# A graph network kernel: the halves of an edge chunk are taken from the two halves of the edge list, each stream of writes waits only for its own, and 23 chunks instead of 30 stand beside the sort

## The reference, cut to what matters

```python
def _L0_gnn_ref(h, row, col, Wq, bq, ...):          # row = src, col = dst
    q = (h @ Wq + bq) * scaling; k = h @ Wk + bk; v = h @ Wv + bv   # 8 heads of 32
    s = einsum('ehd,ehd->eh', q[row], k[col])
    p = exp(s - segment_max(s, row)[row])
    attn = p / segment_sum(p, row)[row]
    return segment_sum(attn[:, :, None] * v[col], row).reshape(n, 256) @ Wo + bo

def _L1_gnn_ref(vertex_features, edge_features, edge_index, W1, ...):
    aggr = segment_sum(edge_features, edge_index[1], num_segments=6250)   # by dst
    h = relu(concatenate([vertex_features, aggr], -1) @ W1 + b1)
    h = relu(h @ W2 + b2)
    return h @ W3 + b3

x = x + _L0_gnn_ref(relu(layernorm(x)), src, dst, ...)
x = x + _L1_gnn_ref(relu(layernorm(x)), edge_attr_256, stack([src, dst]), ...)
```

## Time and profile before

| | |
|---|---|
| median of 3 runs | 1761.8 us (1758.71 to 1763.22) |
| the profiled execution's own time | 1765.26 us |
| its span in the profile | 1763.4 us |
| busy share of the span | PE 82%, DVE 79%, POOL 54%, ACT 44% |
| granted TensorE clock, mean | 0.915 |
| moved by DMA | 431.44 MB, mean 245 GB/s |

### The profile page before, as it was taken

How to read it: one execution, slowest core, us unless ns; L and a number is a source line. 1 busy time by engine, 2 the same in 40 slices (tenths; PEclk the granted TensorE clock), 3 DMA queues, 4 the chain that set the end, 5 groups by cost and what they waited for, 6 DMA issues and landing times.

```text
span 1763.4 us, 26250 instructions
## 1 busy us (share of the span) xinstructions
PE 1450.6 (82%) x7084; PEld 893.7 (51%) x7084; DVE 1394.7 (79%) x2414; ACT 774.4 (44%) x2475; POOL 958.9 (54%) x1021
## 2 busy tenths in 40 slices
PE   4998989965788888877888787876799987778998
PEld 4544444433455555544555455544566655545555
DVE  9998777756777877777878677867898998987785
ACT  5844444445456455545555455520122211115553
POOL 7044444366667666666666566665777777740000
PEclk9999999968989889898989888888999998889999
DMA  9634666688879888889889788876899977763552
GB/s 226 108 117 160 209 210 212 208 281 306 304 262 315 287 291 309 302 297 308 296 274 314 268 299 291 285 239 174 259 300 326 296 250 233 225 199 114 176 176 81
DMA packets 222986, 431.44 MB, mean 245 GB/s; under 512 B 59848, under 2 KB 133135, under 8 KB 222831
## 3 DMA queue, kind: packets, MB, share of 16 engines
q0 software_dynamic: 68832, 225.25, 39.5%
q1 hardware_dynamic: 132073, 132.41, 25.1%
q10 hardware_dynamic: 21926, 72.01, 11.0%
HBM read 376.73 MB, written 52.74 MB: 244 GB/s over the span
## 4 chain that ended last, share of the span: by engine, by line
DMA 46%; PE 23%; SPq 9%; issue 8%; DVE 5%; POOL 5%; ACT 3%; DVEq 0%; ACTq 0%; POOLq 0%
DMA ag_rows<-R 40%; SPq L601 5%; PE bank L1718 4%; POOL U L966 4%; DMA U<-kv_rows,dstb 2%; PE bank L1944 2%; PE bank L1932 2%; PE bank L1782 2%; SPq L603 2%; PE bank L1533 2%; DMA EBO<-in_edge_attr_dram 2%; PE bank_pair L1919 1%; PE bank L1499 1%; PE bank_pair L1702 1%; ACT R L1071 1%
## 5 line engine op out<-in xcount | busy, mean ns | idle before, releaser
L966 POOL DMA_INDIRECT U<-kv_rows,dstb x856 | 810.5, 947 | 398.1 <-issue 217.8
L1718 PE MATMUL bank<-V 128*128 128x264 f32 x1712 | 464.5, 413 | 6.6 <-DVE V L2598 5.5
L1718 PEld LDWEIGHTS bank<-V 128*128 128x128 f32 x1712 | 343.1, 206 | 89.5 <-issue 25.9
L2540 DVE TENSOR_TENSOR V<-U,bank_pair 128x1024 f32<-128x1024 f32 x214 | 259.6, 1213 | 53.9 <-DMA U<-kv_rows,dstb 32.8
L1533 PE MATMUL bank<-EBO 128*64 128x256 f32 x1568 | 251.4, 426 | 23.6 <-DMA EBO<-in_edge_attr_dram 18.1
L2549 DVE TENSOR_REDUCE V<-V 128x32 f32<-128x1024 f32 x214 | 259.2, 1211 | 2.0
L2598 DVE TENSOR_TENSOR V<-U,bank 128x1024 f32<-128x1024 f32 x214 | 258.6, 1208 | 1.4 <-ACT bank L1287 1.3
L1151 ACT ACTIVATE EBO<-iota,dA 128x64 f32<-128x64 f32 x664 | 217.4, 343 | 27.7 <-PE bank L1533 20.4
L1702 PE MATMUL bank_pair<-V 128*128 128x256 f32 x428 | 165.0, 472 | 71.7 <-DVE V L2540 42.7
L1159 ACT ACTIVATE EBO<-EBO,ones 128x64 f32<-128x64 f32 x544 | 189.3, 348 | 17.7
L945 POOL TENSOR_SCALAR EBO<-iota,dA 128x64 f32<-128x64 f32 x120 | 103.2, 880 | 147.7 <-PE bank L1533 147.7
(11 more groups left out here) (260 smaller groups left out, 2054.7 us busy)
## 6 DMA issues: line engine op xcount, KB each, us to landing
EBO<-in_edge_attr_dram ACTq DMA_DIRECT2D x133, 512.0 KB, 7.1
EBO<-in_edge_attr_dram SPq DMA_DIRECT2D x62, 512.0 KB, 3.8
U<-kv_rows,dstb POOLq DMA_INDIRECT x856, 5.3
kv_rows<-U SPq DMA_DIRECT2D x49, 256.0 KB, 2.3
ag_rows<-R SPq DMA_DIRECT2D x196, 64.0 KB
V<-q_rows SPq DMA_DIRECT2D x54, 128.0 KB, 6.2
w_rows<-V SPq DMA_DIRECT2D x54, 128.0 KB, 5.4
V<-slot_places SPq DMA_DIRECT2D x52, 128.0 KB, 8.0
```

What stands on the lines that cost most here:

```text
L966: e.indirect_dma_start(out=kvb[:, b % n, j, :], out_offset=None, in_=kv_dram[:, :], in_offset=bass.IndirectOffsetOnAxis(ap=dstb[:, k:k + 1 ...
L1718: t = e.matmul(o[:, 0:RW], ohog[b % NPV], PVg[b % NPV][:, j, :, :].rearrange("p h d -> p (h d)"), start=first and j == 0, stop=y == SG - 1 ...
L2540: e.tensor_tensor(Tg, kvb[:, b % NKG, :, 0:D], qv, ALU.mult).then_inc(b_mult, 1)
```

## The change

The two halves of chunk c used to be neighbours in the edge list, halves 2c and 2c+1. Now they are half c and half c+98, one from each half of the edge list. A write now waits only for the write before it of its own stream: `s_ag[i]`, which then counts the chunks. Both writes of a chunk are issued one behind the other, at one place in the program. The one place where the two streams meet, window 98, is mended by a copy: SP reads its 64 rows back once (after the eighth chunk, into `seam_rows`), and writes them again at the end (`seam`). DVE computes one more flag for it (four small instructions and a memset in `beside_turn`, n = 3), and the chunk masks and PE's transposes of `l2B` follow the new numbering. The `F2` semaphores now count by chunk parity.

The planner's `STEP` goes from 0.25 to 0.27 and `ALONE` from `ET + 14` to `ET + 21`, and `AGG0` is no longer rounded to 16 steps. That gives `AGG0` = 184, so 23 chunks beside the sort. The 75 others run in the rounds b = 2 to 151, and `AE` becomes 153; what is placed by `AE` (the far rows, the border sums, the products of the sums with W1 from `YB` on) moves back by 14 rounds.

```diff
-        STG, TILE, STEP, TURN, BACK, AHEAD, LATE = 1.38, 3.72, 0.25, 1.9, 1.0, 6.5, 0.4
+        STG, TILE, STEP, TURN, BACK, AHEAD, LATE = 1.38, 3.72, 0.27, 1.9, 1.0, 6.5, 0.4
-        ALONE = ET + 14
+        ALONE = ET + 21
+        SEAM = 8
-        AGG0 = min(at[1], AGG_STEPS) // 16 * 16
+        AGG0 = min(at[1], AGG_STEPS)
...
+        def half(c, i):
+            return c + NCH * i
+
-        def agg_out(e, c, i):
-            h = 2 * c + i
+        def agg_out(e, c):
             e.wait_ge(a_ev, c + 1)
-            if h:
-                e.wait_ge(s_ag[1 - i], 16 * (c + i))
-            r = e.value_load(base2i[0:1, h:h + 1], min_val=0, max_val=NP)
-            z = R2[c % 2][i * LO:(i + 1) * LO, :]
-            e.dma_start(ag_dram[bass.ds(r, LO), :], z).then_inc(s_ag[i], 16)
-            if h == 0:
-                e.wait_ge(pl.s, F2Z)
-            e.dma_start(F2[c:c + 1, i, :], z[LO - 1:LO, :]).then_inc(s_f2[i], 16)
+            for i in range(2):
+                if c:
+                    e.wait_ge(s_ag[i], 16 * c)
+                r = e.value_load(base2i[0:1, half(c, i):half(c, i) + 1], min_val=0, max_val=NP)
+                z = R2[c % 2][i * LO:(i + 1) * LO, :]
+                e.dma_start(ag_dram[bass.ds(r, LO), :], z).then_inc(s_ag[i], 16)
+                if c == i == 0:
+                    e.wait_ge(pl.s, F2Z)
+                e.dma_start(F2[c:c + 1, i, :], z[LO - 1:LO, :]).then_inc(s_f2[c % 2], 16)
+
+        def seam(e, write):
+            e.wait_ge(s_ag[1 - write], 16 * (NCH if write else SEAM + 1))
+            r = e.value_load(base2i[0:1, NCH:NCH + 1], min_val=0, max_val=NP)
+            rows_ = ag_dram[bass.ds(r, LO), :]
+            if write:
+                e.wait_ge(s_seam, 16)
+                e.dma_start(rows_, seam_rows).then_inc(s_seam, 16)
+            else:
+                e.dma_start(seam_rows, rows_).then_inc(s_seam, 16)

         def agg_outs(e, k):
             c, j = divmod(k, 8)
-            if j == 2 and c >= 2:
-                agg_out(e, c - 2, 1)
             if j == 6 and c:
-                agg_out(e, c - 1, 0)
+                agg_out(e, c - 1)
+            if k == 8 * (SEAM + 2):
+                seam(e, 0)
             if k == AGG_STEPS - 1:
-                agg_out(e, c - 1, 1)
-                agg_out(e, c, 0)
-                agg_out(e, c, 1)
+                agg_out(e, c)
+                seam(e, 1)
```

More of the change, by code:

```diff
@@ L205, in gnn_kernel @@
         lim = eqFL[:, 0:NHF]
-        lb2 = l2B[:, :].rearrange("p (c i) -> p i c", i=2)
         low = padneg.bitcast(F32)[:, 0:NCH * 8]
@@ L284, in gnn_kernel @@
         rowb = WP.take(2)
-        cT2 = WP.take(3)
+        cT2 = WP.take(4)
         ixf = WP.take(4)
@@ L318, in gnn_kernel @@
         Mk2 = FB.take(2, NHF)
+        seam_rows = FB.take(D)[0:LO, :]
         assert FC * FP * FJ == E
@@ L402, in gnn_kernel @@
         lid_ready, l2_ready, flags_ready = sem("lid_ready"), sem("l2_ready"), sem("flags_ready")
+        s_seam = sem("s_seam")
         a_ohp, a_oha, a_half, a_ev = sem("a_ohp"), sem("a_oha"), sem("a_half"), sem("a_ev")
@@ L464, in agg_bank @@
             if c < C0:
-                return bank[6 + c % 2][:, 0:D]
+                return bank[6 + (C0 - c) % 2][:, 0:D]
             return bank[5 if grouped and (c - C0) % 2 else 6][:, 0:D]
@@ L580, in nth, with agg_load @@
             return b // n + 1 - (b % n < VB)
+        def half(c, i):
+            return c + NCH * i
         def edge_col(c, j):
-            return (2 * c + j % 2) * 4 + j // 2
+            return half(c, j % 2) * 4 + j // 2
         def half_rows(h):
             return LASTP if h == LH else P
[L588 to L591, removed]
+        def agg_load(e, m):
+            c, i = divmod(m, 2)
+            if c < NCH:
+                if m >= NEB:
+                    e.wait_ge(a_half, m - NEB + 1)
+                h = half(c, i)
@@ L1518, in agg_sum @@
             def agg_sum(c, j, grouped):
-                i, h = j % 2, 2 * c + j % 2
-                n = half_rows(h)
+                i, m = j % 2, 2 * c + j % 2
+                n = half_rows(half(c, i))
                 if j < 2:
-                    e.wait_ge(s_eb[h % NEB], 16 * (h // NEB + 1))
+                    e.wait_ge(s_eb[m % NEB], 16 * (m // NEB + 1))
                 if onehot_on_pool(c, j):
@@ L1532, in agg_sum @@
                         e.wait_ge(p_qr, NT)
-                m = e.matmul(agg_bank(c, grouped)[i * LO:(i + 1) * LO, :], oh2[c % 2][0:n, j, :], eb[h % NEB][0:n, j // 2, :],
+                t = e.matmul(agg_bank(c, grouped)[i * LO:(i + 1) * LO, :], oh2[c % 2][0:n, j, :], eb[m % NEB][0:n, j // 2, :],
                              start=j < 2, stop=j >= 6)
                 if j >= 6:
-                    m.then_inc(a_half, 1)
+                    t.then_inc(a_half, 1)
             turns = 0
@@ L1637, in span_turns @@
                         e.transpose(bank[3][:, o:o + NH], v[:, blk * P:(blk + 1) * P], ident[0:NH, 0:NH])
-                for i in range(2):
-                    e.transpose(bank[3][0:NCH, 160 + i * NH:160 + (i + 1) * NH], lb2[0:NH, i, :], ident[0:NH, 0:NH])
-                e.transpose(bank[3][0:NCH - 1, 160 + 2 * NH:160 + 3 * NH], lb2[0:NH, 0, 1:NCH],
-                            ident[0:NH, 0:NH]).then_inc(span_out, 1)
+                for i, (a, n) in enumerate(((0, NCH), (NCH, NCH), (1, NCH), (NCH + 1, NCH - 1))):
+                    t = e.transpose(bank[3][0:n, 160 + i * NH:160 + (i + 1) * NH], l2B[0:NH, a:a + n], ident[0:NH, 0:NH])
+                t.then_inc(span_out, 1)
             def row_places(p):
@@ L1667, in far_rows @@
                 for i in range(2):
-                    e.wait_ge(s_f2[i], 16 * NCH)
+                    e.wait_ge(s_f2[i], 32 * ((NCH + 1 - i) // 2))
                 for i in range(2):
@@ L2079, in beside_turn @@
                     dv.on(e.tensor_tensor(lim[:, 0:LH], lim[:, 0:LH], l2B[:, 1:NHF], ALU.min))
-                    dv.on(e.tensor_scalar(bad[:, 3:4], l2B[:, LH:NHF], float(N - LO), None, ALU.is_lt))
+                    step(e.tensor_scalar(bad[:, 3:4], l2B[:, LH:NHF], float(N - LO), None, ALU.is_lt))
+                    step(e.tensor_tensor(bad[:, 1:2], l2B[:, NCH + SEAM + 1:NCH + SEAM + 2], l2B[:, NCH:NCH + 1], ALU.subtract))
+                    step(e.tensor_scalar(bad[:, 1:2], bad[:, 1:2], float(LO), None, ALU.is_lt))
+                    step(e.tensor_tensor(bad[:, 3:4], bad[:, 3:4], bad[:, 1:2], ALU.max))
+                    dv.on(e.memset(bad[:, 1:2], 0.0))
                 elif n == 4:
```

23 lines of the change are left out of this document (12 added, 11 removed).

## The result

The changed kernel takes 1600.5 us (median of 4 runs, 1597.8 to 1601.7) against 1760.3 us of the kernel before (4 runs, 1753.3 to 1763.2): a ratio of 0.910, 95% interval 0.907 to 0.913. The profiled execution has a span of 1599.8 us.

The account below looks back on a forecast made before the run. Serial window writes, delaying SP's loads, were taken to bound sort and edge-sum rounds, POOL's gathers the later rounds. Span 1151.3 + 4 + 311.9 + 187.4 = 1654.6, then + 1.9 − 3.5 = 1653 us; range 1618 to 1708.

Parts of the forecast that it names:

- Step 1: Sort: PE's lists between turns get shorter, so DVE waits less for transposes; 33 us less, bounds 20 to 37.
- Step 2: Rounds with edge sums: SP no longer waits for writes, slot places come earlier; 151 rounds at 5.35 us, where 137 took 5.90.
- The landing, 8.6 us: Rounds with edge sums: time from issue to landing of the slot places' load, taken between 9.2 and 8.0 us.
- The issue, 9.0 us: Rounds with edge sums: SP issues the slot places' load 9.0 us after the start of y = 1, before 10.3.
- rival A: Rounds with edge sums: places land within 7.3 us, POOL's gathers set 5.01 us a round; 1602 us, chance 0.12.
- step 3: The stop behind the edge sums, near round 153: 4 us in place of 10.5, ends 0 and 12.
- step 4: Rounds 153 to 215, without edge sums: 62 rounds at 5.03 us, 311.9 us, as before.
- Rival B: Rounds with edge sums: transfers become the bound at 314 GB/s; 1676 us, or 1695 to 1733; chance 0.22 together with D.
- Rival C: Rounds with edge sums: places' load lands later behind two writes and a query load; 1781 us at 12 us landing; chance 0.04.
- D: Rounds with edge sums gain nothing, DVE waits for places as before, only the sort gains; 1736 us, chance 0.22 with Rival B.
- Steps 4 and 5: Rounds 153 to 215, 311.9 us as before; then from round 215 to the end of the span, 187.4 us, not touched.

## Why the prediction was wrong, step by step

**Step 1, the sort: right.** Forecast: 33 us less, waits for the transposes about 16 us. DVE's waits, 160 to 330 us:

```profile
DVE U L2148 <- PE bank_pair L1567: 6.4, 6, 1.7
DVE U L2127 <- PE bank_pair L1567: 4.7, 6, 1.3
DVE dstb L2193 <- PE bank_pair L1567: 1.9, 1, 1.9
```

13.0 us against 48.9, round 2 34 us earlier. The two halves of the change do not add up there, as the experiments show.

**Step 2, the rounds with edge sums: the mechanism right, two terms of its sum mis-sized, above all the landing.** The wait for places did follow SP's backlog, and it went with it. The forecast put the places at 9.0 + 8.6 = 17.6 us after the start of y = 1, where DVE arrives at 14.8. In the mean over the groups of the changed kernel the load was issued at 8.1 and landed 6.2 later, at 14.3 (before 11.6 and 8.4, at 20.0), and DVE, which arrives at 15.3, waited 0.5 us.
- *The landing, 8.6 us, is the step that failed most.* It was taken between two rows of before, 9.2 and 8.0. In the kernel before nearly every one of these loads was issued behind ACT's edge loads; which transfers it would stand behind after the change was not asked. Ahead of them its median is 5.8 us; put behind them again it is 8.4, and the time is 1698 us. The trace of before had it: its three loads issued ahead of both edge loads (518.5, 847.6 and 917.6) took 5.7, 7.1 and 7.7. Put right alone, this term brings the forecast's own group to POOL's floor: 9.0 + 6.2 = 15.2, a wait of 0.4, 19.0 us, under 20.0.
- *The issue, 9.0 us.* "This place is set by PE and DVE, not by the writes, so I keep it": that sentence failed too. The evacuation at 3.36 us was itself a result of the wait, by way of PE's idle time and the clock, and came at 2.5. The granted clock at 719 to 724 was not asked for. Alone, 8.1 in place of 9.0 leaves a wait of 1.9 and a group of 20.5, 5.1 us a round, some 1619 us by the forecast's sum.

Both errors went one way. The sum named the landing's threshold, 7.3 us, and its worth, and gave rival A 0.12. Rival A is what happened, 1602 us by its sum; the distance of 1.25 us between gathers bounds rounds at 5.01. The forecast was 0.37 us a round too high (5.35 less 4.98), 56 us in 151 rounds, and 2 us too high in the sort; step 3 and step 4 give 4 us of it back. The sum's text also has SP no longer waiting for writes: it still does, 104.2 us where it was 371.3, only not with the places late behind it.

**Rival B, bytes: refuted** as it was stated. 314 GB/s (316 in the 100 us from 1290 on) was no limit. It came of POOL's own rate in a stretch without edge sums and their loads; with edge sums the same engines moved 347 over 680 us. The Trainium skill, "DMA: Bandwidth & Descriptors", section Specifications, gives about 358 GB/s as the HBM limit of a core; the 347 stay below it. **Rival C, slower, and D:** neither. The load did stand right behind two writes and a query load, and landed sooner, not later. (C's "2.6 us that it is issued earlier" is no difference of the rows it shows, 10.3 and 9.0; it is that of 9.0 to 11.6, the mean of all groups.)

**Step 3, the stop behind the edge sums: size right, place other.** POOL doesn't stop there (0.8 us at most). DVE does, once, for PE and ACT:

```profile
1108.07 1.22 DVE L2559 TENSOR_TENSOR V<-U,bank_pair 128x1024 f32<-128x1024 f32 x1 [5.14 <-ACT V L1331]
```

From round 153 to 215 it is 319.8 us, 7.9 over 62 × 5.03, where 4 were forecast.

**Steps 4 and 5: right,** 187.3 us at the end.

**What is shown and what not.** Shown: with the writes waiting for each other the 150 us of waiting for places are back and the whole gain is gone, so it needs the separate waits, all but the 15 us that the planner gives by itself; on top of them the planner is worth 13 us; a load of 128 KB that comes later and behind two edge loads costs 98 us. Not parted: how much of the 98 is the order of the transfers and how much SP's wait. Read from the trace alone: that POOL's issue is the floor on the first chip. POOL's timeline leaves no gap, but PE (89% busy), DVE (91%) and the transfers (a share of 0.97) may stand just below it; this was not measured there, since the kernels with fewer gathers or fewer bytes never ran on that chip.

## What to carry to other kernels

When a wait goes, every time of the old trace that lies behind it is in question, the clock and the order of transfers too: ask of each row that you keep whether the wait itself made it. A floor that is named with a threshold close to the forecast (here 8.6 us against 7.3) is worth more than 12 in 100, above all if both inputs come from the congested state. A gain measured on one chip need not hold on the next: read there as well how often the engine that should bind stands still.

## What the hardware showed unexpectedly

On three of the four chips POOL issues a gather every 1.56 us in the mean (257 in the 400 us of the changed kernel's stretch there), on the first every 1.25, though it is busy 0.95 us for each on both. There it issues at most 12 in a row, and then all stand (on the first chip the changed kernel has hundreds in a row). "remote" stands where the view finds no instruction that gave the signal. The changed kernel on such a chip; POOL's last gather of such a row and its next, PE, DVE and ACT:

```profile
644.26 0.95 POOL L983 DMA_INDIRECT U<-kv_rows,dstb  x1 [0.30 <-issue]
650.37 0.95 POOL L983 DMA_INDIRECT U<-kv_rows,dstb  x1 [5.16 <-DVE V L2617]
```

```profile
638.10 0.23 PE L1767 MATMUL bank<-ident,V 128*32 128x32 f32 x2
...
640.62 0.38 PE L1743 MATMUL bank_pair<-ident,attn 128*128 128x128 f32 x2
```

```profile
647.61 0.47 DVE L2597 TENSOR_TENSOR_SCAN V<-V,bank 32x160 f32<-32x160 bf16 x1 [6.17 <-remote]
```

```profile
647.76 0.37 ACT L1323 COPY cTn<-bank_pair 128x256 f32<-128x256 f32 x1 [9.09 <-remote]
```

DVE waits for PE's L1767, which by its record ended at 638.3, and ACT for L1743, which ended at 641.0. Both start at 647.6 to 647.8, 2.4 us after POOL's last gather ended; in other places it is 1.7 to 2.8. It looks as if signals were held while gathers go out one after the other, but this is a guess: neither fewer bytes nor fewer rows changed the time, only fewer gathers did, and no run here made POOL pause or its rows much shorter. The cause stays open.
